# The bias of the experts' first layer as a matmul of two rows

## The reference, cut to what matters

```
# x: 10000 x 512; the layer normalisation of x is h
m    = relu([h[src], edge_attr] @ W1.T + b1) @ W2.T + b2        # edges
gi   = segment_sum(m, dst) @ W_ih.T + b_ih
gh   = h @ W_hh.T + b_hh                                        # 512 -> 3 x 512
r, z = sigmoid(i_r + h_r), sigmoid(i_z + h_z)
n    = tanh(i_n + r * h_n)
x1   = x + h + bn((1 - z) * n + z * h)

h2      = layernorm(x1)
logits  = h2 @ Wg + bg                                          # 8 experts
w, sel  = softmax(top_2(logits)), their indices
hid     = relu(h2 @ W1_e + b1_e)                                # 8 x 32
out     = sum over the two chosen e of w_e * (hid_e @ W2_e + b2_e)
        + 0.5 * (relu(h2 @ Ws1 + bs1) @ Ws2 + bs2)
result  = x1 + out
```

## Time and profile before

| | |
|---|---|
| median of 3 runs | 1486.32 us (1485.1 to 1486.37) |
| the profiled execution | 1488.01 us |
| its span, first to last instruction | 1486.2 us |
| mean granted TensorE clock | 0.98 |
| busy: PE, PEld, DVE, ACT, POOL | 1400.7, 1138.9, 1109.3, 609.7, 926.5 us |

### The profile page before, as it was taken

How to read it: one execution, slowest core, us unless ns; L and a number is a source line. 1 busy time by engine, 2 the same in 40 slices (tenths; PEclk the granted TensorE clock), 3 DMA queues, 4 the chain that set the end, 5 groups by cost and what they waited for, 6 DMA issues and landing times. The chain is left out here.

```text
span 1486.2 us, 23121 instructions
## 1 busy us (share of the span) xinstructions
PE 1400.7 (94%) x6780; PEld 1138.9 (77%) x6780; DVE 1109.3 (75%) x2777; ACT 609.7 (41%) x1100; POOL 926.5 (62%) x1049
## 2 busy tenths in 40 slices
PE   4699999999679999999999999999999999999995
PEld 3578888877457888888888888888888888888884
DVE  3475444234278888888888888888888888888885
ACT  3341212201244445444445444454444454444441
POOL 3210250302178787878787877878788878787771
PEclk9899999999889999999999999999999999999997
DMA  8312333345522223332223222233322223322220
GB/s 215 124 52 91 113 116 123 104 123 149 176 92 98 88 93 103 100 103 93 90 97 102 99 96 91 96 101 103 103 93 90 94 102 100 103 92 91 96 91 28
DMA packets 77137, 152.92 MB, mean 103 GB/s; under 512 B 34842, under 2 KB 36744, under 8 KB 76979
## 3 DMA queue, kind: packets, MB, share of 16 engines
q0 software_dynamic: 45056, 79.02, 16.7%
q1 hardware_dynamic: 32048, 73.48, 15.2%
HBM read 115.67 MB, written 36.66 MB: 103 GB/s over the span
## 5 line engine op out<-in xcount | busy, mean ns | idle before, releaser
L1453 PE MATMUL bank<-whh_hi,h_hi 128*125 128x512 f32 x960 | 391.7, 408 | 22.2 <-DVE h_lo L486 22.2
L1453 PE MATMUL bank<-whh_hi,h_lo 128*125 128x512 f32 x960 | 379.5, 395 | 0.0
L1453 PE MATMUL bank<-whh_lo,h_hi 128*125 128x512 f32 x960 | 378.2, 394 | 0.0
L1453 PEld LDWEIGHTS bank<-whh_hi,h_hi 128*125 128x125 f32 x960 | 178.8, 186 | 60.1 <-DVE h_lo L486 22.6
L1453 PEld LDWEIGHTS bank<-whh_hi,h_lo 128*125 128x125 f32 x960 | 178.3, 186 | 44.6
L1453 PEld LDWEIGHTS bank<-whh_lo,h_hi 128*125 128x125 f32 x960 | 178.8, 186 | 37.9
L1210 POOL DMA_INDIRECT gates<-gates_in,slot_at x80 | 129.7, 1622 | 78.3 <-POOL slot_at L1208 65.4
L1291 ACT ACTIVATE hn_raw<-bank 125x512 f32<-125x512 f32 x80 | 47.8, 598 | 270.6 <-PE bank L1453 270.6
L1249 POOL TENSOR_TENSOR h_n<-h,n_gate 125x512 f32<-125x512 f32 x80 | 103.8, 1297 | 59.5 <-ACT n_gate L1319 59.5
L1235 POOL TENSOR_TENSOR hn<-hn_raw,hn_bias 125x512 f32<-125x512 f32 x80 | 104.1, 1301 | 31.0 <-ACT hn_raw L1291 30.9
L1262 POOL TENSOR_TENSOR x_h_b<-x_h,bn_shift 125x512 f32<-125x512 f32 x80 | 104.2, 1303 | 20.8 <-ACT x_h L479 18.0
(11 more groups left out here) (176 smaller groups left out, 3290.0 us busy)
## 6 DMA issues: line engine op xcount, KB each, us to landing
xt<-in_x SPq DMA_DIRECT2D x80, 250.0 KB
out<-y SPq DMA_DIRECT2D x80, 250.0 KB
gates_in<-g_out SPq DMA_DIRECT2D x16, 750.0 KB
wih_lo_raw<-in_wih_t SPq DMA_DIRECT2D x4, 768.0 KB, 24.9
whh_lo_raw<-in_whh_t SPq DMA_DIRECT2D x4, 768.0 KB, 11.8
gates_in<-late_out SPq DMA_DIRECT2D x6, 250.0 KB
gates_in<-g_out SPq DMA_DIRECT2D x6, 250.0 KB
gates<-gates_in,slot_at POOLq DMA_INDIRECT x80, 10.8
```

The costliest lines, as they stand in the source:

```text
L1453: last = pe.matmul(to[0:R, :], a[:, s, k * R:(k + 1) * R], w[:, k, q * D:(q + 1) * D], start=n == 0, stop=n == 3 * DK - 1)
```

## The change

The 296 biases are read into two partitions (`bias_raw`, both rows alike) instead of 125. Ahead of the node stage DVE makes `bias_rows` of them: row 0 is the hi part, row 1 the lo part. `ones_rows` is two rows of ones. In each turn a thirteenth matmul, ones_rows (2 x 125) times bias_rows (2 x 296), opens the sum in `b_f1`; it stands behind PE's wait for h2_lo and in front of the twelve. L1386 and `f1` are gone: the routing and the next turn's L1351 and L1355 read `b_f1` itself. The bank is therefore in use until `hid` is done in the next turn, and PE waits for `hid_done` instead of `f1_done`. Two tiles used once, `f2_last` and `f2_last_hi`, move to the place of `ig_bias`.

```diff
+            pool.memset(two_ones[:, :], 1.0).then_inc(bias_sign, 1)
+            pool.iota(minus_is_lo[:, :], pattern=[[0, 1]], base=0, channel_multiplier=-1,
+                      allow_small_or_imprecise_dtypes=True).then_inc(bias_sign, 1)
...
+            dve.wait_ge(bias_sign, 2)
+            dve.tensor_copy(ones_rows[:, :], two_ones[:, :]).then_inc(bias_rows_done, 1)
+            dve.wait_ge(bn_back, 16 * (2 + len(rows_of_biases)))
+            dve.tensor_copy(bias_hi[:, :], bias_raw[:, :]).then_inc(bias_hi_done, 1)
+            dve.wait_ge(bias_hi_done, 1)
+            dve.scalar_tensor_tensor(bias_rows[:, :], bias_hi[:, :].bitcast(F32), minus_is_lo[:, 0:1], bias_raw[:, :],
+                                     ALU.mult, ALU.add).then_inc(bias_rows_done, 1)
...
-                    dve.tensor_scalar(extra[:, 0:HS], f1[:, NE + HE:F1], 0.0, 0.5, ALU.max, ALU.mult)\
+                    dve.tensor_scalar(extra[:, 0:HS], b_f1[0:R, NE + HE:F1], 0.0, 0.5, ALU.max, ALU.mult)\
...
-                        f1[:, NE:NE + HE].rearrange("p (e f) -> p e f", e=NE), 0.0,
+                        b_f1[0:R, NE:NE + HE].rearrange("p (e f) -> p e f", e=NE), 0.0,
...
-                    dve.wait_ge(f1_prod, t)
-                    dve.tensor_tensor(f1[:, :], b_f1[0:R, 0:F1], f1_bias[:, :], ALU.add).then_inc(f1_done, 1)
-                    dve.wait_ge(f1_done, t).then_inc(held["dve"], 1)
-                    dve.max(top[:, :], f1[:, 0:NE]).then_inc(top_done, 1)
+                    dve.wait_ge(f1_prod, t).then_inc(held["dve"], 1)
+                    dve.max(top[:, :], b_f1[0:R, 0:NE]).then_inc(top_done, 1)
...
-                    dve.max_index(top_i[:, :], top[:, :], f1[:, 0:NE]).then_inc(top_i_done, 1)
+                    dve.max_index(top_i[:, :], top[:, :], b_f1[0:R, 0:NE]).then_inc(top_i_done, 1)
...
                     pe.wait_ge(h2_lo_done, t)
-                    wait_from(pe, f1_done, t - 1)
+                    wait_from(pe, hid_done, t - 1)
+                    pe.matmul(b_f1[0:R, 0:F1], ones_rows[:, 0:R], bias_rows[:, :], start=True, stop=False)
                     n = 0
                     for k in range(DK):
                         for a, w in ((h2_hi, f1_hi), (h2_hi, f1_lo), (h2_lo, f1_hi)):
                             last = pe.matmul(b_f1[0:R, 0:F1], a[:, k * R:(k + 1) * R], w[:, k, :],
-                                             start=n == 0, stop=n == 3 * DK - 1)
+                                             start=False, stop=n == 3 * DK - 1)
```

More of the change, by code:

```diff
@@ L85, in gnn_ffn @@
     ones_col = place("ones_col", [R, SUP])
+    two_ones = place("two_ones", [2, P])
+    ones_rows = place("ones_rows", [2, P], F32R)
+    minus_is_lo = place("minus_is_lo", [2, 1])
+    bias_rows = place("bias_rows", [2, F1], F32R)
     iota8 = place("iota8", [R, NE])
@@ L94, in gnn_ffn @@
     hn_bias = place("hn_bias", [R, D])
-    f1_bias = place("f1_bias", [R, F1])
+    bias_raw = place("bias_raw", [2, F1])
     region_f = cursor[0]
@@ L186, in gnn_ffn @@
     group_paired = place("group_paired", [R, NSUP, SUP, SUP])
-    f2_last = place("f2_last", [P, D])
-    f2_last_hi = place("f2_last_hi", [P, D], F32R)
+    f2_last = nc.alloc_sbuf_tensor_at("f2_last", [P, D], F32, offset=region_bias)
+    f2_last_hi = nc.alloc_sbuf_tensor_at("f2_last_hi", [P, D], F32R, offset=region_bias + 4 * D)
+    bias_hi = nc.alloc_sbuf_tensor_at("bias_hi", [2, F1], F32R, offset=region_bias + 8 * D)
     region_e = cursor[0]
@@ L226, in gnn_ffn @@
     f2_step = sem("f2_step")
+    bias_sign = sem("bias_sign")
+    bias_hi_done = sem("bias_hi_done")
+    bias_rows_done = sem("bias_rows_done")
     is_lo_step = sem("is_lo_step")
@@ L284, in gnn_ffn, with bcast @@
         (hn_bias[:, :], b_hh[2 * D:G3]),
-        (f1_bias[:, 0:NE], bg), (f1_bias[:, NE:NE + HE], eb1), (f1_bias[:, NE + HE:F1], bs1),
+        (bias_raw[:, 0:NE], bg), (bias_raw[:, NE:NE + HE], eb1), (bias_raw[:, NE + HE:F1], bs1),
     ]
-    def bcast(v):
-        return v.rearrange("(o n) -> o n", o=1).broadcast_to((R, v.shape[0]))
+    def bcast(v, rows=R):
+        return v.rearrange("(o n) -> o n", o=1).broadcast_to((rows, v.shape[0]))
     FIRST, UNROLL = 4, 4
@@ L331, in gnn_ffn @@
     h2_lo = place("h2_lo", [P, DK * R], F32R)
-    f1 = place("f1", [R, F1])
     hid = place("hid", [R, 2, KF * P])
@@ L385, in gnn_ffn @@
     f1_prod = sem("f1_prod")
-    f1_done = sem("f1_done")
     top_done = sem("top_done")
@@ L577, in _ @@
                     for to, of in rows_of_biases:
-                        sp.dma_start(to, bcast(of)).then_inc(bn_back, 16)
+                        sp.dma_start(to, bcast(of, to.shape[0])).then_inc(bn_back, 16)
                     sp.wait_ge(bn_out, 16)
@@ L1483, in body @@
                     pe.wait_ge(f_lo_done, 3)
+                    pe.wait_ge(bias_rows_done, 2)
                 if p.has(-1):
                     pe.wait_ge(h2_lo_done, t)
-                    wait_from(pe, f1_done, t - 1)
+                    wait_from(pe, hid_done, t - 1)
+                    pe.matmul(b_f1[0:R, 0:F1], ones_rows[:, 0:R], bias_rows[:, :], start=True, stop=False)
                     n = 0
```

## The result

The changed kernel takes 1499.9 us (median, 1498.48 to 1501.45) against 1485.84 of the kernel before in the same comparison: 1.0096 times as long, 95% interval 1.0083 to 1.011. It is slower; the forecast was 1484.4 with a range up to 1493. The profiled execution took 1498.48 us with a span of 1496.7.

The account below looks back on a forecast made before the run. PE's 12.82 us loop plus a 0.33 us stall for DVE's h2_lo was taken to bound each turn. 76 turns x -0.02 = -1.5 us and drain -0.4 gave -1.9 us: 1484.4 us, range 1476 to 1493.

Parts of the forecast that it names:

- What bounds the kernel: Node stage: a turn of 13.15 us is PE's own 12.82 plus a 0.33 us wait for DVE's h2_lo.
- the price of the added matmul: PE, experts' product: the thirteenth matmul of 296 columns adds 0.14 us a turn, bounds 0.10 and 0.33.
- the stall does not cover it: PE: the new matmul stands behind the wait for h2_lo, so its 0.14 us adds to PE's loop, giving 12.96.
- Rival (d): PE: thirteenth matmul costs 0.24 us or has its weights laid bare; +7 to +14 us, 1493 us; chance 0.12.
- The subtraction L1391: DVE: held until POOL's h_n ends, median 0.6 to 0.8 us; of 0.62 us removed only 0.07 are left.
- The alternation: Node stage: turns with L1363 held by POOL's L1235 (13.29 us) alternate with free ones (12.96), mean 13.13.
- No cost for the changed wait, the reads of the bank, the set-up: Waiting for hid_done, DVE reading PSUM (bounds 0.00 to 0.03 us for two operations) and one-time set-up all cost nothing.
- (a): Rival: POOL does not hold L1391, PE alone sets 12.96 us a turn; -14.4 us, 1471.5 us; chance 0.08.
- (b): Rival: L1235 slips and two free turns follow each other, a third held, 13.07 us a turn; 1480 us; chance 0.17.
- (c): Rival: bank reads or a newly held DVE operation delay L1363, up to all turns held; 1490 us together; chance 0.17.

Follow-up runs that it names:

- experiment 5: Changed kernel with the two-row bias matmul behind the twelve matmuls instead of in front: 1505.41 us, 1.0129 times the kernel before.
- experiment 1: Changed kernel with the bias matmul widened from 2 rows to 128, the added ones rows being zeros: 1487.4 us, 1.0004 times the kernel before.
- experiment 2: Changed kernel with the bias matmul left out, so the result lacks that bias: 1480.02 us, 0.9953 times the kernel before.
- experiment 7: On top of experiment 1, the subtraction of the two greatest logits as a tensor_scalar with one tensor input: 1481.62 us, 0.9962 times the kernel before.

## Why the prediction was wrong

**What bounds the kernel** stands. The period was 13.15, PE's own loop 12.82; adding 0.52 to it gives 13.34, and the changed kernel has 13.36 with only a quarter of the turns held.

**The step that failed** is the price of the added matmul: "I take 0.14, because 296 columns are what the neighbours pass", with 0.10 and 0.33 as bounds. It measured 0.52. The 0.14 was right for the columns (0.13 with 65 or 128 rows). What was missing is the step between 64 and 65 rows: with two rows the load does not start under the matmul before it, and neither does the load behind it. The upper bound allowed for one load laid bare, at one border; there are two borders, together 0.39 us.

A second sentence failed with it: "the stall does not cover it". In the changed kernel's held turns the second of the twelve stands 1.13 us behind the transposes, in its free turns 0.98: PE waits 0.15 us, not 0.33, because the first border (0.17) lies within the wait. With the two rows behind the twelve (experiment 5), where it can't, the wait is 0.38.

Rival (d), the dear matmul, was the case that came, at a chance of 0.12 and a price of 1493, 7 us too low. That it came so near is in part luck: the surplus was 0.38 us a turn where (d) allowed for 0.10 to 0.19, and the stall, which (d) kept at 0.33 in half of the turns, shrank to 0.15 in a quarter.

The row that misled was the smooth spacing of 0.14: it was measured between matmuls of 125 or 128 rows, and the trace of before holds no other kind. The Trainium skill's rule on changing modes (TensorEngine Tiling (Array Packing), section Tiling Modes), without a price there, was a reason to ask; the prediction did not draw on it.

**The subtraction L1391** took over the hold, as forecast: 0.44 us in the median, ending with h_n (0.6 to 0.8 was forecast; the dearer matmul brings the product, and the start, later; with 128 rows the median is 0.67). z_h_n follows h_n by 0.28, as forecast.

**The alternation** was right in the count: with the matmul at 0.13 (experiment 1) half of the turns are held. But the turn is 13.20 against 13.13 forecast, 1487.4 us against 1484.4. The stall of a held turn was mis-sized, because only L1363 had been looked at and not the cast in front of it. The mean distance (us) from the transposes to the second of the twelve, 600 to 1400 us, shows it:

| | free turn | last hid operation held | cast held |
|---|---|---|---|
| before | 0.46 | 0.82 | |
| experiment 2, no matmul | 0.46 | | 1.01 |
| experiment 1, 128 rows | 0.59 | 1.00 | 1.20 |
| changed kernel, 2 rows | 0.98 | 1.13 | |

(The first 0.46 is from a turn near the end; between 600 and 1400 us the kernel before has no free turn.) A held turn of experiment 1 thus waits 0.41 or 0.61 us, not 0.33. With 17 and 13 such turns of 60, the estimate is 12.96 + 0.25 = 13.21. For experiment 2 it is 12.82 + 0.28 = 13.10, as measured; by the prediction's 0.33 it would have been 12.98. Why the first of the two is 0.41 and not 0.33 was not looked into.

**No cost for the changed wait, the reads of the bank, the set-up**: consistent with experiment 2, which has them all and is faster than before. The 0.13 us that the prediction worked out from the Trainium skill (VectorE: DVE Perf Modes, the section on the TRN2 errata) for L1351 and L1355 does not show: in the changed kernel, from the bank, they mean 183 and 424 ns; with SBUF inputs they were 179 and 425.

**Rivals**: (a) is out, L1391 is held. (b) did not come as meant: in the changed kernel fewer turns are held than half, but because PE's loop grew. (c), all turns held, did not come; the newly held operation that it allowed for exists, though: the cast, in 13 turns of experiment 1. (d) came.

## What to carry to other kernels

Before adding a small matmul to a stream, compare its rows (the contraction) with its neighbours': here 2 or 64 rows between matmuls of 125 and 128 cost 0.39 us a time more than the same product padded with zero rows, so pad. (Putting several such products side by side might share the two borders; no run shows it.) A price read off a row holds for a neighbour of the same kind; where the new operation differs in one of its sizes, the bound has to be taken as if nothing overlapped, at both ends. And when an operation is removed from an engine whose operations another engine's work can hold, look for every operation that comes to lie there, not only the one that is held now: 0.62 us off DVE left 0.06, until the subtraction and the order around hn were changed too.

## What the runs showed of the hardware that I had not expected

The step between 64 and 65 rows: 0.98 us against 0.59 from the transposes to the second of the twelve, with nothing in between. And how fine the order of DVE and POOL is: missing POOL's hn by 0.02 to 0.07 us holds a 0.2 us operation of DVE for 1.3 us, in nearly half of the turns of experiment 7. Where an input lies decides too: the same tensor_scalar of 32 columns, started while POOL's x_h_b runs, takes 0.67 us from SBUF and 0.18 from the bank.
